# Last cross attention: 32 distances per row, slanted through DRAM, in one pipeline of 32 units, in place of two groups with per-query relative terms

## The reference

```
q = heads(x @ Wq)                       # 16 batches, 128 rows, 16 heads of 64
k, v = heads(ctx_t @ Wk), heads(ctx_t @ Wv)          # 77 text positions
sim = einsum('bihd,bjhd->bhij', q, k) * SCALE
dist = clip(arange(77)[None, :] - arange(128)[:, None], -16, 16) + 16
sim = sim + einsum('bihd,ijd->bhij', q, rel_k[dist]) * SCALE
attn = softmax(sim)
out = einsum('bhij,bjhd->bihd', attn, v) + einsum('bhij,ijd->bihd', attn, rel_v[dist])
out += stream(Wk_ip, Wv_ip, ctx_i) * (tanh(alpha) + 1)    # 16 positions, a softmax of its own
out += stream(Wk_ap, Wv_ap, ctx_a) * (tanh(beta) + 1)     # 35 positions, a softmax of its own
x = x + out @ Wo + bo                   # x went in through a layer norm
```

## Time and profile before

| what | us |
|---|---|
| median of 3 runs | 2702.07 |
| lowest and highest | 2699.56, 2702.21 |
| span of the profiled execution | 2747.7 |
| stage l3x in it, 2230.8 to 2664.2 | 433.4 |
| TensorE busy in that stage | 404.4 |

### The profile page before, as it was taken

How to read it: one execution, slowest core, us unless ns; L and a number is a source line. 1 busy time by engine, 2 the same in 40 slices (tenths; PEclk the granted TensorE clock), 3 DMA queues, 4 the chain that set the end, 5 groups by cost and what they waited for, 6 DMA issues and landing times. The chain is left out here.

```text
span 2747.7 us, 48070 instructions
## 1 busy us (share of the span) xinstructions
PE 2425.4 (88%) x18022; PEld 1804.3 (66%) x18024; DVE 1424.7 (52%) x3052; ACT 1135.2 (41%) x2771; POOL 737.6 (27%) x839
## 2 busy tenths in 40 slices
PE   7989869999797989769999799997899989899885
PEld 5767655665575977636666378886465658868772
DVE  5767402223564867612222456665665736515748
ACT  4468422222675635412222333333764643313415
POOL 4556241111353531040111111222101112201325
PEclk9999779999898999779999899998899999999998
DMA  5000442114101100331111500002000021202200
GB/s 177 2 2 2 188 180 62 45 46 174 63 2 49 47 1 2 143 134 74 46 45 37 217 1 1 1 1 93 1 1 1 1 85 55 70 0 70 62 3 31
DMA packets 61439, 152.34 MB, mean 55 GB/s; under 512 B 8974, under 2 KB 36750, under 8 KB 56145
## 3 DMA queue, kind: packets, MB, share of 16 engines
q1 hardware_dynamic: 52094, 122.23, 12.9%
q0 software_dynamic: 9120, 27.04, 2.7%
HBM read 101.46 MB, written 47.78 MB: 54 GB/s over the span
## 5 line engine op out<-in xcount | busy, mean ns | idle before, releaser
L3782 POOL TENSOR_TENSOR l3x_Pn<-l3x_Pn,l3x_fac 128x616 f32<-128x616 f32 (+2 forms) x96 | 70.3, 761 | 286.7 <-DVE l3x_fac L3832 286.7
L2108 POOL TENSOR_TENSOR l2a_Pn<-l2a_Pn,l2a_rden 128x1024 f32<-128x1024 f32 x32 | 60.1, 1897 | 295.5 <-DVE l2a_rden L2350 295.5
L1678 DVE TENSOR_TENSOR l1f_work<-l1f_work,l1f_psU 128x512 f32<-128x512 f32 x55 | 37.8, 687 | 191.8 <-PE l1f_psU L1426 167.0
L1442 PE MATMUL l1f_psY<-l1f_W,l1f_hT 128*128 (+1 forms) x440 | 106.1, 385 | 25.6 <-ACT l1f_hT L1539 25.6
L1533 ACT ACTIVATE l1f_work<-l1f_psG 128x512 f32<-128x512 f32 x55 | 32.8, 597 | 213.3 <-PE l1f_psG L1419 190.7
L1442 PEld LDWEIGHTS l1f_psY<-l1f_W,l1f_hT 128*128 128x128 f32 x440 | 81.4, 193 | 42.6 <-ACT l1f_hT L1539 26.5
L1351 POOL DMA_INDIRECT results_by_token<-l1f_rows_in_out,l1f_dest x39 | 37.4, 959 | 265.0 <-DVE l1f_rows_in_out L1689 265.0
L1351 POOL DMA_INDIRECT results_by_token<-l0f_rows_in_out,l0f_dest x39 | 37.2, 955 | 230.4 <-DVE l0f_rows_in_out L1689 230.4
L1678 DVE TENSOR_TENSOR l0f_work<-l0f_work,l0f_psU 128x512 f32<-128x512 f32 x39 | 26.8, 687 | 128.2 <-PE l0f_psU L1426 128.2
L885 ACT ACTIVATE l1a_att_Pn<-l1a_att_psS,l1a_att_nmx 128x128 f32<-128x128 f32 x256 | 91.8, 418 | 1.7 <-DVE l1a_att_nmx L1004 1.7
L885 ACT ACTIVATE l0x_Pn<-l0x_psS,l0x_nmx 128x128 f32<-128x128 f32 x256 | 91.7, 418 | 0.9 <-DVE l0x_nmx L1004 0.9
(11 more groups left out here) (784 smaller groups left out, 7128.2 us busy)
## 6 DMA issues: line engine op xcount, KB each, us to landing
l1f_W<-in_l1f_w SPq DMA_DIRECT2D x9, 1536.0 KB, 19.7
l0f_W<-in_l0f_w SPq DMA_DIRECT2D x8, 1536.0 KB
rows_by_expert<-zeros SPq DMA_DIRECT2D x2, 5011.5 KB, 26.7
l3x_K<-keys SPq DMA_DIRECT2D x16, 512.0 KB, 4.0
values<-l1f_W SPq DMA_DIRECT2D x11, 512.0 KB
l0f_rows_in_out<-rows_by_expert SPq DMA_DIRECT2D x39, 128.5 KB, 2.1
l1f_rows_in_out<-rows_by_expert SPq DMA_DIRECT2D x39, 128.5 KB, 2.1
l3x_V<-values SPq DMA_DIRECT2D x16, 308.0 KB
```

The lines of the kernel that those rows point to most:

```text
L1442: ins = nc.tensor.matmul(psY[:, 0:D], hT[n % 2][:, j * P:(j + 1) * P], weights(n, 2 * DC * F + j * D, D), start=(j == 0), stop=(j == FC - 1))
L1678: nc.vector.tensor_tensor(h[n % 2], sg[n % 2], psU[:, :], ALU.mult).then_inc(h_ready, 1)
L2108: nc.gpsimd.tensor_tensor(part, part, rden[b % 2][:, 8 * u:8 * u + 8].unsqueeze(2).to_broadcast([P, 8, P]), ALU.mult)\
L3782: nc.gpsimd.tensor_tensor(v, v, fac[n % 3][:, s * HH:(s + 1) * HH].unsqueeze(2).to_broadcast([P, HH, SEG[s]]), ALU.mult)\
```

## The change

The two groups become one pipeline of 32 units. Instead of 77 relative terms for each query row, `relative_keys` makes 32 products for each row (the 32 shifted distances, `rkd`, which is `rel_k` less its first column); the constant part drops out of the softmax. ScalarE writes them into an extended row of 168 values per head: 76 zeros, the 32 values, and the last one repeated 60 times (`ext`). SP stores the first 92 rows to DRAM (`relative_rows`, G.RD) and reads them back with a row step one element shorter than the row, so that row i starts i elements earlier: that turns distances into positions (`rel`, 92 x 8 x 77). VectorE adds them to the scores in PSUM.

For the values, VectorE's scan makes running sums of the exponentials along each segment (`cum`), from which it also takes the denominators. SP stores 92 rows of them (`cumulative_rows`, G.CD) and reads back, with a row step one element longer, the 32 running sums around each row's own position (`near`, 92 x 8 x 32). GpSimd masks and scales them, TensorE transposes them, and two products with a table of differences of `rel_v` (`steps`) add the relative values into the outputs. The constant row of `rel_v` goes through Wo once, into the bias (`end_rows`).

Projections of queries and outputs are spread over the units, and x is added and its statistics taken batch by batch. The output bias is added by GpSimd in the first 16 units, and the steps of quantising the next weights stand in the last ones.

The products with the identity are gone from the unit; narrow ones and a share of both projections have come in. The diff, cut to its core:

```diff
-    rk, rv = R.sb("rel_k", [P, P - 1 + SEG[0]]), R.sb("rel_v", [SEG[0], (NREL + 1) * W])
-    RP = R.sb("rel_or_weights", [P, GB * H * P])
...
+    PT = [R.sb(f"PT{i}", [P, HH * P]) for i in range(2)]
+    ext = [R.sb(f"ext{i}", [P, HH * EXT]) for i in range(2)]
+    NR = 3
+    rel = [R.sb(f"rel{i}", [P, HH * S0]) for i in range(NR)]
+    cum = [R.sb(f"cum{i}", [P, HH * P]) for i in range(2)]
+    near = [R.sb(f"near{i}", [P, HH * BAND]) for i in range(2)]
+    nearw = [R.sb(f"nearw{i}", [P, HH * BAND]) for i in range(2)]
+    nearT = [R.sb(f"nearT{i}", [P, 2 * ROWS]) for i in range(2)]
...
+        def near_weights(n):
+            i = n % 2
+            sp.wait_ge(sums_ready, n + 1)
+            past(sp, near_loaded[i], 16 * (n // 2))
+            sp.dma_start(G.CD[i, EDGE:].rearrange("(r e) -> r e", e=HH * P), cum[i][0:ROWS, :]).then_inc(cum_stored[i], 16)
+            sp.wait_ge(cum_stored[i], 16 * (n // 2 + 1))
+            past(sp, near_masked, n - 1)
+            past(sp, near_ready, n - 1)
+            slanted = bass.AP(tensor=G.CD.tensor, offset=G.CD[i, EDGE - MAXREL:].offset, ap=[[HH * P + 1, ROWS], [P, HH], [1, BAND]])
+            sp.dma_start(near[i][0:ROWS, :].rearrange("p (h d) -> p h d", h=HH), slanted).then_inc(near_loaded[i], 16)
+
+        def relative_scores(n):
+            i = n % 2
+            sp.wait_ge(ext_ready, 2 * (n + 1))
+            if n >= 2:
+                sp.wait_ge(rel_loaded[(n - 2) % NR], 16 * ((n - 2) // NR + 1))
+            sp.dma_start(G.RD[i].rearrange("(r e) -> r e", e=HH * EXT), ext[i][0:ROWS, :]).then_inc(ext_stored[i], 16)
+            sp.wait_ge(ext_stored[i], 16 * (n // 2 + 1))
+            past(sp, biased, n - NR + 1)
+            slanted = bass.AP(tensor=G.RD.tensor, offset=G.RD[i, ROWS - 1:].offset, ap=[[HH * EXT - 1, ROWS], [EXT, HH], [1, S0]])
+            sp.dma_start(rel[n % NR][0:ROWS, :].rearrange("p (h j) -> p h j", h=HH), slanted).then_inc(rel_loaded[n % NR], 16)
+
...
+        for it in range(-4, UN):
+            if it % 2 == 0 and it + 4 < UN:
+                load_keys((it + 4) // 2)
+            if it % 2 and it >= -1 and it + 1 < UN:
+                load_values((it + 1) // 2)
+            if it == -1:
+                sp.wait_ge(edge_stored, 32)
+            if 0 <= it + 1 < UN:
+                near_weights(it + 1)
+            if it + 4 < UN:
+                relative_scores(it + 4)
+            if it == UN - 8:
+                sp.wait_ge(q_done, UN)
                 sp.dma_start(S.w[0], A["l3f_W1"]).then_inc(S.loaded[0], 16)
-            if b == GB + 2:
                 sp.dma_start(S.w[1], A["l3f_W2"]).then_inc(S.loaded[1], 16)
...
     @block.tensor
+        def end_rows():
+            pe.wait_ge(small_loaded, NSMALL)
+            pe.wait_ge(out_loaded, 16)
+            for j in range(IC):
+                ins = nc.tensor.matmul(psO[:, 0:D], rve[:, :], wo[:, j * D:(j + 1) * D], start=(j == 0), stop=(j == IC - 1))
...
+        def relative_keys(n, it):
+            b, jj = unit(n)
+            if n == 0:
+                pe.wait_ge(tables_ready, 1)
+            pe.wait_ge(q_taken, 4 * (n // 4) + 4)
+            past(pe, ext_ready, 2 * n)
+            past(pe, pt_taken, it + 1)
+            for l in range(4):
+                for half in range(2):
+                    ins = nc.tensor.matmul(psT[0:ROWS, half * 512 + l * BAND:half * 512 + (l + 1) * BAND],
+                                           qTv[rows(half), b % RING, 4 * jj + l, 0:ROWS], rkd[rows(half), :], start=True, stop=True)
+            ins.then_inc(near_k_done, 1)
...
+        def scores(n):
-            for half in range(2):
-                for l in range(4):
-                    o = (2 * (n % 2) + half) * 512 + l * P
-                    ins = nc.tensor.matmul(psS[:, o:o + SEG[0]], RPv[0:SEG[0], b, half * HH + 4 * jj + l, :],
-                                           G.ident[0:SEG[0], 0:SEG[0]], start=False, stop=(l == 3))
...
+        def transpose_near(n):
+            pe.wait_ge(near_ready, n + 1)
+            pe.wait_ge(pt_taken, min(n + 2, UN))
+            for t in range(2):
+                ins = nc.tensor.transpose(psT[:, NT0 + t * ROWS:NT0 + (t + 1) * ROWS], nearw[n % 2][0:ROWS, t * P:(t + 1) * P],
+                                          G.ident[0:ROWS, 0:ROWS])
+            ins.then_inc(nt_done, 1)
...
+        def weigh(n):
...
+            pe.wait_ge(nt_taken, n + 1)
+            for r in range(2):
+                ins = nc.tensor.matmul(psO[:, :].rearrange("p (t r i) -> p t r i", t=2, r=2)[:, :, r, 0:ROWS], steps[:, r * P:(r + 1) * P],
+                                       nearT[n % 2][:, :].rearrange("p (t i) -> p t i", t=2), start=False, stop=(r == 1))
...
+        for it in range(-8, UN + 2):
+            if 0 <= it < UN:
+                transpose_p(it)
+            if 0 <= it + 2 < UN:
+                scores(it + 2)
+            if it % 2 and it >= 3:
+                project_out((it - 3) // 2, it)
+            if 0 <= it - 1 < UN:
+                transpose_near(it - 1)
+            if 0 <= it + 4 < UN:
+                relative_keys(it + 4, it)
+            if 0 <= it - 1 < UN:
+                weigh(it - 1)
+            if it + 8 < UN:
+                project(it + 8, it)
+            if it == -5:
+                end_rows()
 
...
     @block.scalar
+        def extend(n):
+            i = n % 2
+            act.wait_ge(near_k_done, n + 1)
+            past(act, ext_stored[i], 16 * (n // 2))
+            band = psTv[0:ROWS, :, 0:4 * BAND].rearrange("p s (l d) -> p s l d", l=4)
+            nc.scalar.activation(extv[i][0:ROWS, :, :, ZERO:SAT], band, ACT.Copy).then_inc(ext_ready, 1)
+            nc.scalar.activation(extv[i][0:ROWS, :, :, SAT:EXT], band[:, :, :, BAND - 1:BAND].to_broadcast([ROWS, 2, 4, EXT - SAT]), ACT.Copy)\
+                .then_inc(ext_ready, 1)
...
     @block.gpsimd
+        def near_values(n):
+            i = n % 2
+            pool.wait_ge(near_loaded[i], 16 * (n // 2 + 1))
+            v = near[i][0:ROWS, :].rearrange("p (h d) -> p h d", h=HH)
+            nc.gpsimd.tensor_tensor(v, v, inside[0:ROWS, :].unsqueeze(1).to_broadcast([ROWS, HH, BAND]), ALU.mult).then_inc(near_masked, 1)
+            pool.wait_ge(near_masked, n + 1)
+            past(pool, nt_done, n - 1)
+            pool.wait_ge(f_ready, n + 1)
+            f = fac[n % 3][0:ROWS, 0:HH].rearrange("p (s l) -> p s l", s=2)
+            for s in range(2):
+                ins = nc.gpsimd.tensor_tensor(nearw[i][0:ROWS, :].rearrange("p (l s d) -> p s l d", s=2, l=4)[:, s],
+                                              near[i][0:ROWS, :].rearrange("p (s l d) -> p s l d", s=2, l=4)[:, s],
+                                              f[:, s].unsqueeze(2).to_broadcast([ROWS, 4, BAND]), ALU.mult)
+            ins.then_inc(near_ready, 1)
...
     @block.vector
+        def maxima(n):
+            dve.wait_ge(rel_loaded[n % NR], 16 * (n // NR + 1))
+            v = seg(psS[0:ROWS, (n % 2) * 1024:(n % 2 + 1) * 1024], 0)
+            nc.vector.tensor_tensor(v, v, rel[n % NR][0:ROWS, :].rearrange("p (h k) -> p h k", h=HH), ALU.add).then_inc(biased, 1)
+            dve.wait_ge(biased, n + 1)
...
+        def factors(n):
+            past(dve, cum_stored[i], 16 * (n // 2))
+            nc.vector.tensor_tensor_scan(cum[i][:, :], segments_begin[:, :], Pn[n % NP][:, :], 0.0, ALU.mult, ALU.add).then_inc(sums_ready, 1)
+            dve.wait_ge(sums_ready, n + 1)
+            for s in range(3):
+                step.sig(nc.vector.reciprocal(den[i][:, s * HH:(s + 1) * HH], seg(cum[i][:, :], s)[:, :, SEG[s] - 1]))
...
+        for it in range(-2, UN + 2):
+            if 0 <= it + 1 < UN:
+                factors(it + 1)
+            if it + 2 < UN:
+                maxima(it + 2)
+                subtract(it + 2)
+            if it % 2 and it >= 3:
+                add((it - 3) // 2)
+            if it % 2 == 0 and it >= 4:
+                row_stats((it - 4) // 2)
```

More of the change, by code:

```diff
@@ new lines, in row_stats @@
+        def row_stats(b):
+            xb = G.x[:, b * D:(b + 1) * D]
+            dve.wait_ge(x_ready, b + 1)
+            step.sig(nc.vector.bn_stats(out=st6[:, b * 6:(b + 1) * 6], in_=xb))
+            step.sig(nc.vector.tensor_reduce(G.xmax[:, b:b + 1], xb, AX.X, ALU.max))
+            step.do(nc.vector.tensor_reduce(G.xmin[:, b:b + 1], xb, AX.X, ALU.min))
+            step.sig(nc.vector.bn_aggr(out=G.mv[:, b * 2:b * 2 + 2], in_=st6[:, b * 6:(b + 1) * 6]))
+        for it in range(-2, UN + 2):
[8 more added lines that the diff above has]
+                row_stats((it - 4) // 2)
+            if it in (UN - 7, UN - 6):
+                i = it - (UN - 7)
+                dve.wait_ge(S.loaded[i], 16)
+                for half in range(2):
@@ L3888, in _ @@
[L3888 to L3889 removed]
+            if it == UN - 5:
+                dve.wait_ge(S.wtop_ready, 1)
+                step.do(nc.vector.tensor_tensor(S.sw[:, :], S.wtop[:, 0:2], S.wtop[:, 2:4], ALU.max))
```

(2 more changed lines are left out.)

410 lines of the change are left out of this document (177 added, 233 removed).

## The result

The changed kernel takes 2904.4 us (median of 4 runs, 2898.1 to 2905.9) against 2702.1 for the kernel before on the same chip (4 runs, 2699.6 to 2702.5): a ratio of 1.075, 95% interval 1.073 to 1.076. It is 202 us slower. The forecast was 3080 with a range of 2800 to 3420: the sign and the cause held, the time lies in the range, and it was 176 us under the forecast.

A forecast was written before the change was run, and what follows sets the result against it. TensorE bound the stage before; after, SP's DMA chain on four engines would, at 24.5 us a round. Start 12.5, rounds 40 + 710 + 37, tail 9, weights 5 gave 813.5 against 433.4: +380 on 2702, forecast 3080 us, range 2800 to 3420.

The forecast's parts named there:

- full rounds: Pipeline: 29 rounds with all four transfers, their waits and K and V, 24.5 us each, 710 us.
- Four engines: DMA of the 92-row transfers: 92 = 4 × 23, so each runs on 4 of 16 engines.
- The same four for all: DMA queue: all four transfers of a unit use the same four engines, so their times add to 24.5 us a round.
- the other case: Third rival, DMA: four engines, but not the same four for each transfer; 13.1 us a round, 2714 us, chance 0.08.
- Waits of 1.5 us: SP's queue: from a store's last packet to the held-back load's first, 1.5 us twice a unit, the four engines idle.
- The small pieces: Loads back from DRAM: pieces of 128 B at 25 ns and 308 B at 30 ns, 4.6 and 5.5 us a round.
- the lower line through 8 and 50 ns: Loads back: lower prices, 12 ns at 128 B and 20 ns at 308 B, round 20.3 us, total about 2950 us.
- sixteen-engine and third rivals: DMA: 16 engines share the 92 rows, 2617 us, chance 0.09; four different engines for each transfer, 2714 us, chance 0.08.
- The large rows: Stores to DRAM at 23.4 GB/s an engine: cumulative rows 4.0 us, extended rows 5.3 us a round.
- TensorE 8.4 us a unit, VectorE 7.5: Compute in the pipeline: TensorE 8.4 us and VectorE 7.5 us a unit; stage about 295 us if DMA cost nothing.
- The first rival: DMA: all 16 engines share the 92 rows, 10 us a round, stage 348 us, total 2617 us, chance 0.09.
- the upper prices: Loads back: small pieces at 45 and 81 ns, round 37.4 us, total about 3500 us, chance 0.12.

The follow-up runs named there:

- e7: Changed kernel, same 92 rows, each of the four transfers cut into rows 0 to 79 and 80 to 91: stage 412.5 us, ratio 0.993 to the kernel before.
- e2: Changed kernel with 104 rows in place of 92 in the four transfers: stage 412.6 us, ratio 0.988 to the kernel before.
- e4: Changed kernel, 92 rows, both stores issued first, then each load behind its own store's wait: stage 538.6 us, ratio 1.037 to the kernel before.
- after: The changed kernel itself, 92 rows, SP waiting twice a round: 2904.4 us, stage 637.0 us, ratio 1.075 to the kernel before.
- e9: Changed kernel, 92 rows, both stores issued together and both waited for before either load: stage 582.9 us, ratio 1.056 to the kernel before (one run).
- e3: Changed kernel, both loads reading each row as one straight piece of the same length, result not the reference's: stage 623.7 us, ratio 1.067.
- e5: Changed kernel with 96 rows, both stores issued first, then each load behind its own store's wait: 2608.9 us, ratio 0.967 to the kernel before.
- e1: Changed kernel with 96 rows in place of 92 in the four transfers: stage 381.4 us, ratio 0.981 to the kernel before.
- e10: e5 with ScalarE issuing the exponential of unit it + 2 ahead of the projected queries' copy: 2590.4 us, ratio 0.960 to the kernel before.

## Why the prediction was right in kind and too high in size

The prediction cut the stage into start, rounds with only the bias half, full rounds, values rounds and tail. The trace has the same cuts:

| part | forecast | measured |
|---|---|---|
| start to the first extended store | 12.5 | 12.3 |
| to the first near load (three bias rounds and one cumulative store, 40 + 5.5) | 45.5 | 37.9 |
| 29 full rounds | 710 | 553.7 |
| values rounds and tail (37 + 9 - 5.5) | 40.5 | 33.1 |
| weight loads | 5 | in the rounds (one of them takes 6 us more) |
| stage | 813.5 | 637.0 |

**Four engines: right.** It was the step on which all rested, read from 50 closing packets and a share of 0.68. Closing packets of 4, 2, 16 and 13 a transfer (and 28 a pair in e7), and full rounds of 33.2, 19.1, 11.8 and 10.7 us at 2, 4, 13 and 16 engines, bear it out. What the expectation of e2 got wrong was the divisor of 104, not the rule. By the rule for the number of engines in the Trainium skill (DMA: Bandwidth & Descriptors, section on why a DMA increments its semaphore by 16) the counts are the same; the trace agrees.

**The same four for all: right.** The prediction had no row for it and gave the other case, 2714 us, 0.08. e4's round is the sum of all its transfers, with no overlap among them.

**Waits of 1.5 us, nothing behind them: right.** In after none of the transfers' packets runs from about 2391.95 to 2393.3 and from 2402.3 to 2403.7 (the one packet at 2392.3 loads instructions), 1.35 and 1.4 us, and the first half microsecond after that is slow; e4 took both gaps away (3.4 us of a full round), e9 gave one back (1.4).

**The small pieces: the term that failed.** The prediction took 25 ns for a piece of 128 B and 30 ns for one of 308 B, 4.6 and 5.5 us. Measured are 1.75 / 184 = 9.5 ns and 3.0 / 184 = 16.3 ns. This is 5.35 of the 5.4 us by which the round was too long, times 29 and with the bias and values rounds 171 of the 176 us by which the stage was forecast too long. Even the lower line through 8 and 50 ns gave 12 and 20 ns, with a time "about 2950", so the forecast's own range (2940 to 3330) missed as well; only the sixteen-engine and third rivals stood below it. That the time lies in the stated 2800 to 3420 is no merit of the sum: the low end was set by the chances of those two rivals, whose mechanisms did not come about. The step that went wrong was the choice between two ends: the upper one contained starts and writes of odd rows to DRAM, and I moved the value up from the line toward it without a row that was itself a read of such pieces. The Trainium skill's least size for line rate of 512 B (same page, Specifications) is borne out for the shorter pieces: an engine loads 94.2 KB / 4 / 1.75 us = 13.5 GB/s in pieces of 128 B, against 19.9 in K's rows of 4 KB. In pieces of 308 B it loads 18.9, hardly less than in K's rows. How much of that is the piece and how much the start of a load, e3 leaves open.

**The large rows: 3.6 and 4.7 us for 4.0 and 5.3.** A busy engine stores 108 / (0.26 × 16) = 26 GB/s, not 23.4. The term came out 1.0 us too long. Against this and the pieces stand about 1.2 us that the sum of the parts, 3.6 + 1.35 + 1.75 + 4.7 + 1.4 + 3.0 + 2.1 = 17.9, lacks to 19.1; the 2.1 for K and V is still the forecast's and was not measured by itself. Of the 1.2 the weight loads are 0.2 (6 us over 29 rounds), and the slow first half microseconds behind each gap look like the rest, which no run took apart.

**TensorE 8.4 us a unit, VectorE 7.5: right, and without effect here.** TensorE took 8.0 us in e5. VectorE's scan took 2.39 us (2.32 forecast) and its add 0.80 (0.8). In after TensorE was at half clock in a part of each round, as the prediction allowed, and did not bind.

**The first rival's sum** (16 engines, 10 us a round, stage 348, 2617 us) was close to what the experiments gave once its condition was made true: e1 10.6 us and a stage of 381, e5 9.3 and 338. Against e1 its 32 rounds were 20 us short (10.0 for 10.6) and its start and tail 14 us (27 for 41). It had the two waits in its round; SP still spends 250 of e1's 381 us in them.

**The signs it named.** "A period of 20" was to put the error into the price of small pieces, and the period is 19.1. TensorE is busy for 57% of the stage, not a third, and the DMA share is 0.29, not near 0.2: the round is shorter, and at half clock the same products take longer. The round with the upper prices adds up to 37.6 us, not 37.4.

## What to carry to other kernels

Before a tile goes through DRAM, look at how many rows its transfers have: the count of closing packets, or for long rows the DMA share of one transfer alone, tells how many engines carry it. A full round took 10.7 us at 6 rows an engine, 11.8 at 8, 19.1 at 23 and 33.2 at 47, some 0.5 to 0.6 us for each row more, and 96 rows in place of 92 were worth 256 us of this stage, two more rows in place of 92 cost 450. Where a store must be waited for before a load, issue whatever else is ready first: two idle gaps of some 1.4 us a round, with the slow start behind each, cost 98 us here, and the order of four issues took both away. A change that removes work from the engine that binds has to be read together with what it puts on the queue beside it: here the saving of products was real, and it showed only when the transfers were mended: with 96 rows alone the kernel is 1.9% faster than before, with one turn as well 3.3%, and with the swap of e10 4.0% (2590 us against 2698).
